# Two transformer layers on one core: eight slots for target rows, maxima stored by ScalarE, landed rows loaded by GpSimd, first-layer products placed behind the blocks of column tiles

## What is computed

```
xn = layernorm(x)                                          # layer 0
q, k, v = gelu(xn @ W1 + b1) @ W2 + b2                     # three small MLPs
out = tril(q @ k.T / sqrt(128*256)) @ v                    # no softmax
x1 = x + (layernorm(out) * ln_w + ln_b)
       + fp4(silu(fp4(xn) @ Wg) * (fp4(xn) @ Wu)) @ Wd     # blockwise FP4 quantise/dequantise
xn = layernorm(x1)                                         # layer 1
out = softmax(q_h @ k.T / 8) @ v,  16 query heads, one k and v head;  out @ Wo + bo
moe = 8 experts 128 -> 512 -> 128 with gelu, the top 2 of each token, weighted
x2 = x1 + attention + moe
```

## Time and profile before

| | |
|---|---|
| median of 3 runs | 1470.13 us (1468.08 to 1475.42) |
| profiled execution | 1460.9 us, span 1459.0 us |
| TensorE busy | 1300.1 us, 89% |
| VectorE busy | 1013.9 us, 69% |
| ScalarE busy | 708.1 us, 49% |
| GpSimd busy | 252.5 us, 17% |
| TensorE's granted clock, mean | 0.953 of 2.4 GHz |

### The profile page before, as it was taken

How to read it: one execution, slowest core, us unless ns; L and a number is a source line. 1 busy time by engine, 2 the same in 40 slices (tenths; PEclk the granted TensorE clock), 3 DMA queues, 4 the chain that set the end, 5 groups by cost and what they waited for, 6 DMA issues and landing times.

```text
span 1459.0 us, 22233 instructions
## 1 busy us (share of the span) xinstructions
PE 1300.1 (89%) x7377; PEld 767.7 (53%) x7377; DVE 1013.9 (69%) x2393; ACT 708.1 (49%) x1300; POOL 252.5 (17%) x306
## 2 busy tenths in 40 slices
PE   4569888999999999999999999999998778979877
PEld 2335445555555555555555555555454466656634
DVE  7777776578757875787677767776776456666655
ACT  3136454544454445444545454545454464757531
POOL 3132222201010111011001200110002035242510
PEclk9579999999999999999999999999999899999989
DMA  2042442002000200020002000200003255445242
GB/s 72 14 130 93 128 139 103 31 17 77 24 29 17 82 22 26 17 82 24 24 17 82 26 23 17 82 27 21 16 18 113 78 167 171 135 157 163 72 154 59
DMA packets 72372, 100.26 MB, mean 69 GB/s; under 512 B 29196, under 2 KB 49228, under 8 KB 68292
## 3 DMA queue, kind: packets, MB, share of 16 engines
q1 hardware_dynamic: 59876, 70.69, 15.6%
q0 software_dynamic: 10192, 27.44, 5.8%
q10 hardware_dynamic: 2192, 0.71, 0.2%
HBM read 59.86 MB, written 38.68 MB: 68 GB/s over the span
## 4 chain that ended last, share of the span: by engine, by line
PE 61%; DVE 15%; issue 12%; POOL 6%; DMA 2%; SPq 2%; ACT 1%; DVEq 0%; POOLq 0%; ACTq 0%
PE bank L1423 13%; PE bank L1395 7%; PE bank L1351 6%; PE bank L1396 6%; PE bank L1434 6%; POOL y_rows L701 5%; PE bank L1455 4%; DVE mneg L990 3%; PE bank L1275 3%; PE bank L1259 3%; PE bank L1260 2%; PE bank L1261 2%; PE bank L1310 2%; DVE q_lm L984 2%; PE bank L1292 1%
## 5 line engine op out<-in xcount | busy, mean ns | idle before, releaser
L821 ACT ACTIVATE wide<-bank 128x512 f32<-128x512 f32 x512 | 301.5, 604 | 502.8 <-PE bank L1396 492.5
L990 DVE TENSOR_REDUCE mneg<-bank 128x1 f32<-128x512 f32 x512 | 347.4, 686 | 203.6 <-PE bank L1351 197.7
L1395 PE MATMUL bank<-q_hh,k_hl 128*128 128x512 f32 x512 | 236.2, 461 | 19.8 <-DMA q_lm<-mrow 18.2
L1423 PE MATMUL bank<-wide,v_w 128*32 128x512 f32 x2048 | 248.7, 604 | 0.5 <-issue 0.5
L1351 PE MATMUL bank<-k_hl,q_hh 128*128 128x512 f32 x512 | 208.5, 409 | 36.0 <-DVE mneg L990 22.1
L1396 PE MATMUL bank<-q_lm,k_h 65*128 65x512 f32 x512 | 204.2, 399 | 0.0
L1395 PEld LDWEIGHTS bank<-q_hh,k_hl 128*128 128x128 f32 x512 | 97.7, 191 | 151.6 <-issue 109.4
L1351 PEld LDWEIGHTS bank<-k_hl,q_hh 128*128 128x128 f32 x512 | 98.7, 193 | 73.7 <-issue 52.8
L631 POOL TENSOR_TENSOR rs<-rs,power 128x4 f32<-128x4 f32 x24 | 24.6, 1026 | 626.2 <-DVE rs L892 626.2
L1434 PE MATMUL bank<-wide,ones 128*32 128x512 f32 x992 | 129.1, 592 | 0.0
L701 POOL DMA_INDIRECT y_rows<-y_m,to_u x92 | 92.4, 1004 | 177.0 <-DVE y_m L1117 155.0
(11 more groups left out here) (230 smaller groups left out, 2001.4 us busy)
## 6 DMA issues: line engine op xcount, KB each, us to landing
w_t<-w_rows SPq DMA_DIRECT2D x23, 1024.0 KB
x_rows<-part_h POOLq DMA_DIRECT2D x65, 258.0 KB, 5.7
inv<-inverse_scratch SPq DMA_DIRECT2D x124, 128.0 KB, 3.0
w_rows<-w_t SPq DMA_DIRECT2D x8, 1024.0 KB, 4.9
x_m<-x_rows SPq DMA_DIRECT2D x23, 258.0 KB
stage<-in_L_ffn_W SPq DMA_DIRECT2D x16, 256.0 KB, 4.8
yab<-y_rows SPq DMA_DIRECT2D x8, 512.0 KB, 7.3
xin<-in_L_attn_x SPq DMA_DIRECT2D x8, 256.0 KB, 4.0
```

Of the source, the lines that this page charges most:

```text
L821: act.activation(wide[:, st.g % WIDE, :], ps, ACT.Exp, scale=SCALE1).then_inc(wide_full, 1)
L990: dve.tensor_reduce(mneg[:, (gh // 2) % 2, col:col + 1], ps[:], X, ALU.max, negate=True)\
L1395: pe.matmul(ps, k_hl[:, n, t], q_hh[:, gh % HEADS, :], start=True, stop=False)
L1423: pe.matmul(ps_out[0][rows, :], v_w[:, n, c, TILE * d:TILE * d + TILE], weights, start=(c == 0), stop=(c == TT - 1))
```

## The change

1. `TO` = 8: `to_u` and the semaphores of the result scatter have eight slots, `tile_in(t)` waits for tile t - 8.
2. The rows of a tile are transposed at the first and results at the third step of a tile, before both stood at the second.
3. ScalarE issues the store of the maxima itself, behind its copy, after waiting for the copy; SyncE no longer does.
4. GpSimd loads the landed rows, right behind its last scatter.
5. Row 7: weights of the first four tiles are loaded at k = 1, 5, 10 and 13 rather than all at k = 0; rows of the first two at k = 10 rather than 9.
6. First-layer products stand at k mod 4 = 1 only, which is behind `values`; VectorE's pieces are placed anew; the causal norm's pieces come behind the second quantisation rather than the third, its gain behind the third.
7. The query stands ahead of the maximum's scores in its step, and VectorE's `lo_q` ahead of the first-layer pieces.
8. `xq`, `xqt` and the zeros lie over `part_h`; GpSimd's roots in row 0 stand at other places.

```diff
-    WT, XT, YT, YM = 4, 2, 2, 3
+    WT, XT, YT, YM, TO = 4, 2, 2, 3, 8
-    L0_AT = {1: -8, 2: -7, 3: -5, 4: -5, 5: -3, 6: -2, 7: -1, 8: -1, 9: 1, 10: 2, 13: 2, 14: 3, 15: 4, 16: 4,
-             17: 8, 19: 16, 20: 17, 21: 24, 22: 25, 23: 32, 24: 33, 25: 38, 26: 39, 27: 41}
+    L0_AT = {1: -7, 2: -7, 3: -3, 4: -3, 5: 1, 6: 1, 13: 1, 14: 1, 7: 5, 8: 5, 9: 9, 10: 9, 15: 13, 16: 13, 17: 13,
+             19: 17, 20: 17, 21: 25, 22: 25, 23: 33, 24: 33, 25: 37, 26: 37, 27: 41}
-    L0_DVE = [-14, -11, -11, -10, -7, -6, -4, -2, 0, 0, 9, 10, 13, 17, 18, 21, 25, 26, 29, 30, 30, 31, 32,
-              33, 34, 37, 38, 39, 40, 42, 43, 44, 44]
+    L0_DVE = [-14, -11, -11, -10, -8, -6, -5, -2, 2, 6, 14, 14, 15, 18, 19, 20, 21, 22, 23, 24, 26, 27, 29, 31,
+              34, 34, 35, 38, 40, 42, 43, 44, 44]
-    LANDED_AT = 41
+    ROWS_AT, WEIGHTS_AT = 10, [1, 5, 10, 13]
...
     def tile_events(st):
-        if st.g is None or st.g % TT != 1:
+        if st.g is None:
             return []
-        here = st.g // TT
-        return [(use, tile_of[i]) for use, i in (("tx", here + 1), ("ty", here - 2)) if i in tile_of]
+        here, c = divmod(st.g, TT)
+        use, i = {0: ("tx", here + 1), 2: ("ty", here - 2)}.get(c, (None, None))
+        return [(use, tile_of[i])] if i in tile_of else []
...
         ahead_ = gh + LEAD + s // TT
+        if s % TT == 1 and 0 <= ahead_ + 1 < H * NB:
+            events.append(("q", ahead_ + 1))
         if 0 <= ahead_ < H * NB:
             events.append(("mx", ahead_, s % TT))
         if s == TT + 1 and 0 <= gh + 2 < H * NB:
             events.append(("mt", (gh + 2) // 2))
-        if s % TT == 1 and 0 <= ahead_ + 1 < H * NB:
-            events.append(("q", ahead_ + 1))
...
         def landed(eng, t):
-            eng.wait_ge(y_scattered[t % WT], TT * (t // WT + 1) * 16)
+            eng.wait_ge(y_scattered[t % TO], TT * (t // TO + 1) * 16)
...
                     if st.kind == "o" and st.k == 0:
                         for i in range(WT):
                             sp.wait_ge(w_stored[i], E // WT * 16)
-                        for t in range(WT):
-                            load_tile_weights(t)
-                    if st.kind == "o" and st.k == 9:
+                    if st.kind == "o" and st.k in WEIGHTS_AT:
+                        load_tile_weights(WEIGHTS_AT.index(st.k))
+                    if st.kind == "o" and st.k == ROWS_AT:
                         for t in range(XT):
                             load_tile_rows(t)
...
+            for t in range(TILES - TO, TILES):
+                landed(pool, t)
+            for n in range(NB):
+                pool.dma_start(yab[:, n], y_rows[1 + 2 * S * n:1 + 2 * S * (n + 1), :]
+                               .rearrange("(i p b) d -> p i b d", p=P, b=2)).then_inc(yab_loaded[n], 16)
...
                 act.activation(mrow[:, pair % 2, :], ps[0:2 * TT, 0:P], ACT.Identity).then_inc(free, 1)
+                read_out(act, ("mt", pair))
+                at_ = (2 * pair) % HEADS
+                act.dma_start(q_lm[DK:DK + 1, at_:at_ + 2, :].bitcast(F32), mrow[:, pair % 2, :].bitcast(F32))\
+                   .then_inc(m_loaded[pair % 2], 16)
...
-                if t >= WT:
-                    landed(dve, t - WT)
+                if t >= TO:
+                    landed(dve, t - TO)
...
+                if split_head(st) is not None:
+                    lo_q(split_head(st))
                 if st.kind in ("pre", "o"):
                     for n, k in ((st.r + 1, st.k), (st.r + 2, st.k - ATT)):
                         for _ in range(L0_DVE.count(k) if 0 < n < NB else 0):
                             next(cuts[n], None)
-                if split_head(st) is not None:
-                    lo_q(split_head(st))
```

More of the change, by code:

```diff
@@ L325, in two_layers @@
         hid0, s0t, sg = over("hid0", [P, 3, S], 1), over("s0t", [P, TT, S], 1), over("sg", [P, TT, I0], 1)
-        qk0, xq, xqt = over("qk0", [P, 2, S], 5), over("xq", [P, S], 5), over("xqt", [P, S], 6)
+        qk0 = over("qk0", [P, 2, S], 5)
         hqt = over("hqt", [P, 2, IC, P], 4)
@@ L345, in two_layers @@
         wide = sb("wide", [P, WIDE, S])
-        part_h = sb("part_h", [P, PARTS, S], F32R)
+        part_h_at = nc.sbuf_base + (-nc.sbuf_base) % 64
+        sb("part_h_arena", [P, PARTS * S + 16])
+        part_h = nc.alloc_sbuf_tensor_at("part_h", [P, PARTS, S], F32R, offset=part_h_at)
+        zeros = nc.alloc_sbuf_tensor_at("zeros", [P, TT * ROW], F32, offset=part_h_at)
+        xq = nc.alloc_sbuf_tensor_at("xq", [P, S], F32, offset=part_h_at + 2 * S * 4)
+        xqt = nc.alloc_sbuf_tensor_at("xqt", [P, S], F32, offset=part_h_at + 3 * S * 4)
         part_at = nc.sbuf_base + (-nc.sbuf_base) % 64
@@ L374, in two_layers @@
         b_t = sb("b_t", [P, WT, 8])
-        to_f, to_u = sb("to_f", [P, TT]), sb("to_u", [P, WT, TT], U32)
-        zeros = part_h[:].rearrange("p n s -> p (n s)")[:, 0:TT * ROW].bitcast(F32)
+        to_f, to_u = sb("to_f", [P, TT]), sb("to_u", [P, TO, TT], U32)
         bank = [ctx.enter_context(nc.psum_tensor(f"bank{i}", [P, S], F32)) for i in range(8)]
@@ L406, in two_layers @@
         xm_loaded = [sem(f"xm_loaded{i}") for i in range(XT)]
-        to_set, y_scattered = sem("to_set"), [sem(f"y_scattered{i}") for i in range(WT)]
+        to_set, y_scattered = sem("to_set"), [sem(f"y_scattered{i}") for i in range(TO)]
         yab_loaded = [sem(f"yab_loaded{i}") for i in range(NB)]
@@ L548, in load_tile_rows @@
                   .then_inc(xm_loaded[t % XT], 16)
[L550 to L553, removed]
-                sp.dma_start(yab[:, n], y_rows[1 + 2 * S * n:1 + 2 * S * (n + 1), :]
-                             .rearrange("(i p b) d -> p i b d", p=P, b=2)).then_inc(yab_loaded[n], 16)
             def store_out(n):
@@ L564, in _ @@
             for st in steps:
-                for event in head_events(st):
-                    if event[0] == "mt":
-                        store_m(event[1])
                 for r, k in row_steps(st):
@@ L640, in _ @@
             pool.iota(spare[:], [[S, TILES], [1, TT]], 1 + 2 * TOKENS, TT, allow_small_or_imprecise_dtypes=True).then_inc(consts, 1)
-            pool.memset(part_h[:].bitcast(F32), 0.0).then_inc(consts, 1)
+            pool.memset(zeros[:], 0.0).then_inc(consts, 1)
             pool.wait_ge(split_h, 1)
@@ L700, in _ @@
                 for i in range(TT):
[L701 to L702 removed]
+                    pool.indirect_dma_start(y_rows, bass.IndirectOffsetOnAxis(ap=to_u[:, t % TO, i:i + 1], axis=0),
+                                            y_m[:, t % YM, i, :], None).then_inc(y_scattered[t % TO], 16)
+            for t in range(TILES - TO, TILES):
[3 more added lines that the diff above has]
+                               .rearrange("(i p b) d -> p i b d", p=P, b=2)).then_inc(yab_loaded[n], 16)
         @block.scalar
@@ L922, in l0 @@
                 last_product = next(quantise)
+                if n > 0:
+                    yield last_product
+                    for _ in quantise:
+                        pass
                 yield 6
@@ L935, in l0 @@
                                              SCALE0, causal[:], ALU.mult, ALU.mult).then_inc(free, 1)
-                yield last_product
-                for _ in quantise:
-                    pass
+                if n == 0:
+                    yield last_product
+                    for _ in quantise:
+                        pass
                 def down(i):
@@ L948, in attended, with gain @@
                     yield from norm(v0, v0, link, tag)
+                def gain():
+                    link(dve.tensor_tensor(v0[:], v0[:], wide_(lnw_row), ALU.mult))
+                    link(dve.tensor_tensor(v0[:], v0[:], wide_(lnb_row), ALU.add))
                 if n == 0:
@@ L962, in l0 @@
                     yield from fp4(sg[:, i, :], sg[:, i, :], NBI, lambda ins: ins.then_inc(hq_done, 1), (s, s, None))
+                    if i == 1 and n > 0:
+                        yield from attended(s)
                     if i == 2 and n > 0:
-                        yield from attended(s)
-                yield 24
-                link(dve.tensor_tensor(v0[:], v0[:], wide_(lnw_row), ALU.mult))
-                link(dve.tensor_tensor(v0[:], v0[:], wide_(lnb_row), ALU.add))
+                        yield s
+                        gain()
+                if n == 0:
+                    yield 24
+                    gain()
                 yield 26
```

17 lines of the change are left out of this document (4 added, 13 removed).

## The result

| | before | changed |
|---|---|---|
| median | 1471.0 us | 1488.3 us (1485.63 to 1492.5) |
| ratio | 1 | 1.0118 (95%: 1.008 to 1.0155) |
| profiled execution, span | 1459.0 us | 1490.6 us |
| row 0 / rows 1 to 6 (mean) / row 7 from its first scores to the end | 153.3 / 141.5 / 346.1 us | 161.3 / 152.3 / 306.3 us |
| idle time of TensorE in one row (row 4) | 5.6 us | 11.6 us |

Rows are measured between the first scores of k = 0. Row 6 is shorter than the others in both (131.1 and 143.9), since nothing of a next row is woven into its end. Row 0 starts 1.2 us earlier (109.3), rows 0 to 6 lost 72.6 us and row 7 gained 39.8, which makes the 31.6 us between the spans. By the medians it is 17, since the profiled execution of before lay 10.1 us under its median and that of the changed kernel 4.2 us above.

What follows compares the result with a forecast made beforehand. TensorE was taken to bound the middle rows, DMA waits row 7. From the profiled 1460.9 us, -39 - 1 - 7 - 0 gave 1413.9, plus 9.2 for the median's level 1423 us; range 1384 to 1446.

Steps and rivals of the forecast that it cites:

- Eight slots: Expert tiles in row 7: the wait for an old result's scatter goes; -39 us, bounds -40 and -20.
- Start of row 7: Maxima stored by ScalarE, weights spread: the 11.35 us stall goes, a wait for rows comes; -1 us, bounds -13 and +5.
- the end: Row 7 near k = 48: the maxima's store wait goes, `combine` waits some 2.5 us for landed rows; -7, bounds -10 and 0.
- new wait for `x_m`: Row 7, k = 12: TensorE waits 11.6 us for the rows of tile 0.
- each round trip: Start of row 7: sums' and inverses' trips through DMA, each behind a 1 MB load, take 5.5 us.
- GpSimd's first issue: Near the end of row 7: GpSimd's first issue of the landed rows' loads taken as 0.6 to 2 us.
- Query and ScalarE's issues: Query's new order worth nothing; ScalarE's store issue, 0.68 us once in eight steps, nothing, or 0.7 at most.
- First-layer products: Seven rows, products behind the blocks: 7.2 us of waits removed, 8.1 new; written 0, bounds -5.7 and +2.9 a row.
- the cap of 5.7: TensorE's idle time in a middle row, 5.7 us, is the most that removed waits can give back.
- My count of 8.1 us: New waits a row: 2.1 at k = 17, 1.6 at 19, 2.0 at 37, 1.0 at 61, small places 1.4.
- Rival D: Seven rows: TensorE waits 2 us at each of four VectorE bursts, 8 us a row, 56 in all: 1479; chance 0.04.

Runs made afterwards that it cites:

- slots_alone: The kernel before with parts 1 and 2 alone (eight slots, transposes at a tile's first and third step): 1422.5 us, ratio 0.9727.
- old_first_layer: The changed kernel with part 6 alone undone (first-layer products and VectorE's pieces where they stood before): 1411.9 us, ratio 0.9661 of before.

## Why the prediction was wrong

- **Eight slots, -39**: right, in the number and in the mechanism: slots_alone gives -39.0, and the tiles' stretches are 40.5 us shorter.
- **Start of row 7, -1, and the end, -7**: right in mechanism. Part 3 alone gives 0.0038, -5.6 us, and the new wait for `x_m` was 8.96 us where I had 11.6. I had given each round trip 5.5 us; the sums' took 2.8 behind one load of weights (1193.87 to 1196.68), the inverses' 3.1, and the rows' load went out 25.7 us into the row rather than 32.9. The end kept a wait of 2.05 us, but for the maxima's store, not for `yab`: no wait of `combine` is in the trace. My 0.6 to 2 us for GpSimd's first issue and 3 us for a transfer stood on no row: it issued its eight loads in 6.45 us where SyncE took 7.23, and a load landed in 7.7 us (median) where it took 7.3. The Trainium skill ("DMA: Bandwidth & Descriptors", "Issuing engine by pattern") calls the way of SyncE and ScalarE generally the faster one; for the landing the traces agree, with 7.7 us here and 9.1 in old_first_layer, but TensorE did not wait for it in either. Parts 4 and 5 were not tried alone.
- **Query and ScalarE's issues, 0**: within what the medians can tell, apart from the query's wait at k = 30 of row 7 (3.87 us). The other memory (part 8) was not tried alone, so its 0 is not shown.
- **First-layer products, "I write 0; bounds ... +2.9 a row"**: the step that failed; it measured +10.2 us a row. The removed side was right as far as the cap of 5.7: all the old waits of a row, 5.6 us, went. But the 0 set 8.1 us of new waits against 7.2 removed, which that cap does not allow; by its own count the term was +2.4 a row, +17. And the new side was short by two things. My count of 8.1 us missed places: the trace has 11.6 us in row 4. The exponential at k = 0 is the Gelu of k = 61 that I had at 1.0, but the counts' product of k = 58 (2.2 us) was not in my list. And I priced a wait at its own length. In row 4 the idle time grew by 6.0 us and the row by 10.2; TensorE's busy time grew by 3.9, most of it by its clock. Behind the 2.18 us of k = 58 the same matmul goes from 0.40 to 0.63 us:

```profile
873.43 0.40 PE L1358 MATMUL bank<-k_hl,q_hh 128*128 128x512 f32 x1
873.66 0.51 PE L1402 MATMUL bank<-q_hh,k_hl 128*128 128x512 f32 x1
873.97 0.63 PE L1403 MATMUL bank<-q_lm,k_h 65*128 65x512 f32 x1
874.39 0.63 PE L1358 MATMUL bank<-k_hl,q_hh 128*128 128x512 f32 x1
```

The granted clock falls to the lower level there, 1.2 GHz, and stays for 3.4 us. Row 4 of the changed kernel has three such stretches, from the waits of k = 17, 19 and 58 on:

```profile
774.80:778.20 3.40, 2.86 (x13) 2.86 (x14) 2.34 (x4) 0.00 (x0) 0.00 (x0) 0.50 0.02 5
788.40:791.80 3.40, 3.40 (x12) 1.85 (x14) 3.30 (x10) 2.04 (x4) 0.00 (x0) 0.51 0.05 5
873.80:877.20 3.40, 3.36 (x9) 2.04 (x7) 3.19 (x9) 2.03 (x5) 0.00 (x0) 0.50 0.38 120
```

Row 4 of before has one, behind its longest wait (1.37 us):

```profile
821.50:824.90 3.40, 3.40 (x5) 1.34 (x6) 3.19 (x10) 0.69 (x1) 0.00 (x0) 0.50 0.06 22
```

Two stretches more at half the clock cost 3.4 us; with the 6.0 us of idle time that is 9.4 of the 10.2. I had put this surcharge into the tiles and into the end, and left it out where seven rows multiply it.

- **Rival D** was what happened. I gave it 0.04, although my own count already had more added than removed. Its waits came in different places than "four of 2 us", and not all behind bursts (k = 0 is the Gelu's), but in sum a row was 10.2 us longer against my 8, and it decided from 6.7.

By the ratios: -39.9 us for the slots, -9.6 for parts 3 to 5, 7 and 8 (0.9727 to 0.9661), +66.8 for part 6: +17 in all, where the forecast was -47. The measured 1488.3 us is outside the range, 1384 to 1446, on the side of rival D.

## What to carry to other kernels

Where two engines share a few buffers in rotation, look at how the work of the second lies between the waits of the first, not at its sum: input that comes behind a long block leaves the helper idle through the block and makes it late in the short steps behind it. Price a stall of TensorE with the slow matmuls behind it, here 10.2 us a row for 6.0 us more of waiting, and most carefully in the stage that repeats. When a change has several parts with separate gains, a term written as "0, since +8.1 and -7.2 cancel" is the widest one of the sum, and its sign deserves the rival's chance.

## What the runs showed that I had not expected

A small store behind four queued loads of 1 MB waits above all in the issuing engine's own order: issued by another engine, its wait went from 11.35 to 1.14 us. And single entries of a list of places can matter: two of 33 gave 25 us of 1488, two others nothing.
